# Expert stage of an attention and mixture-of-experts block: the transposes of the next block's rows before the second product instead of inside it

## The reference

```python
gate_probs = jax.nn.softmax(x @ Wg + bg, axis=-1)
_, top_idx = jax.lax.top_k(gate_probs, 2)
...
h = jax.nn.gelu(jnp.einsum('bsf,efh->bseh', x, W1) + b1)
expert_out = jnp.einsum('bseh,ehf->bsef', h, W2) + b2[None, None]
return jnp.einsum('bsef,bse->bsf', expert_out, selected)
```

## Time and profile before

| | |
|---|---|
| median of 3 runs | 966.51 us (966.34 to 971.07) |
| the profiled execution's own time | 965.11 us |
| its span, first to last instruction | 963.4 us |
| mean granted TensorE clock | 0.928 of full |
| PE busy | 825.7 us, 86% of the span |
| DVE busy | 572.3 us, 59% |
| ACT busy | 455.7 us, 47% |
| POOL busy | 276.9 us, 29% |
| chain that ended last, by engine | PE 71%, DVE 12%, POOL 5%, issue 5%, DMA 3% |
| loads of `listed` | 38, of 265.0 KB, 3.0 us to landing (median) |

### The profile page before, as it was taken

How to read it: one execution, slowest core, us unless ns; L and a number is a source line. 1 busy time by engine, 2 the same in 40 slices (tenths; PEclk the granted TensorE clock), 3 DMA queues, 4 the chain that set the end, 5 groups by cost and what they waited for, 6 DMA issues and landing times.

```text
span 963.4 us, 17833 instructions
## 1 busy us (share of the span) xinstructions
PE 825.7 (86%) x5866; PEld 765.9 (80%) x5867; DVE 572.3 (59%) x1365; ACT 455.7 (47%) x876; POOL 276.9 (29%) x206
## 2 busy tenths in 40 slices
PE   5757999999998869864049999999998999999995
PEld 4545888888886757664049999999998999999995
DVE  4768677777777436886016565556656565565553
ACT  4343555665543420111036565747457575665552
POOL 1222223322321012277713222222222222232222
PEclk9979999999998987875569999999999999999998
DMA  8601101101100096643632425152242524322222
GB/s 288 221 0 45 40 5 46 44 1 45 45 1 1 1 348 223 236 153 107 228 108 62 115 40 132 27 132 44 44 131 44 131 44 115 61 45 44 44 45 33
DMA packets 51260, 84.77 MB, mean 88 GB/s; under 512 B 4498, under 2 KB 35668, under 8 KB 51092
## 3 DMA queue, kind: packets, MB, share of 16 engines
q1 hardware_dynamic: 37396, 65.62, 20.1%
q0 software_dynamic: 13824, 18.65, 10.8%
HBM read 50.86 MB, written 33.40 MB: 87 GB/s over the span
## 4 chain that ended last, share of the span: by engine, by line
PE 71%; DVE 12%; POOL 5%; issue 5%; DMA 3%; ACT 1%; SPq 1%; DVEq 0%; ACTq 0%; POOLq 0%
PE ps L1318 20%; PE ps L1306 16%; PE ps L1147 9%; PE ps L1112 8%; PE ps L1166 6%; POOL lists L539 4%; PE ps L1223 3%; PE ps L1156 3%; PE ps L1289 2%; DVE w_lo L1054 2%; DMA listed<-lists 2%; DMA wmod_sb<-in_L_wmod 1%; PE ps L1217 1%; DVE w_lo L1051 1%; DVE ln_s L766 1%
## 5 line engine op out<-in xcount | busy, mean ns | idle before, releaser
L559 POOL DMA_INDIRECT out<-y,y_id x74 | 122.2, 1651 | 349.1 <-DVE y L1043 334.7
L1318 PE MATMUL ps<-w_hi,hid_hi 128*128 128x256 f32 x592 | 171.2, 289 | 12.2 <-DVE hid_lo L1034 12.2
L715 ACT ACTIVATE hid<-ps,b_col 128x256 f32<-128x256 f32 x296 | 122.2, 464 | 113.0 <-PE ps L1306 112.9
L1034 DVE TENSOR_TENSOR hid_lo<-hid,hid_hi 128x512 fp32r<-128x512 f32 x148 | 100.6, 692 | 117.8 <-ACT hid_hi L723 116.4
L1306 PE MATMUL ps<-xT_hi,w_hi 128*128 128x256 f32 x592 | 167.5, 283 | 2.3 <-DVE xT_lo L1015 2.3
L1306 PE MATMUL ps<-xT_lo,w_hi 128*128 128x256 f32 x592 | 167.3, 283 | 0.0
L1306 PE MATMUL ps<-xT_hi,w_lo 128*128 128x256 f32 x592 | 167.2, 282 | 0.0
L1318 PE MATMUL ps<-w_hi,hid_lo 128*128 128x256 f32 x592 | 166.1, 281 | 0.0
L1318 PE MATMUL ps<-w_lo,hid_hi 128*128 128x256 f32 x592 | 166.1, 281 | 0.0
L1318 PEld LDWEIGHTS ps<-w_hi,hid_hi 128*128 128x128 f32 x592 | 112.1, 189 | 15.6 <-DVE hid_lo L1034 14.7
L514 POOL TENSOR_TENSOR q_n<-q_exp,q_rec 128x1024 f32<-128x1024 f32 x32 | 61.0, 1906 | 218.3 <-DVE q_rec L790 218.3
(11 more groups left out here) (190 smaller groups left out, 1491.4 us busy)
## 6 DMA issues: line engine op xcount, KB each, us to landing
w_raw<-in_L_ffn_W SPq DMA_DIRECT2D x16, 1024.0 KB, 8.8
listed<-lists SPq DMA_DIRECT2D x38, 265.0 KB, 3.0
h_store<-h_q SPq DMA_DIRECT2D x8, 1024.0 KB, 4.0
h_b<-h_store SPq DMA_DIRECT2D x16, 512.0 KB, 6.2
x_all<-in_L_attn_x SPq DMA_DIRECT2D x8, 512.0 KB, 11.0
x_b<-in_L_attn_x SPq DMA_DIRECT2D x4, 1024.0 KB, 10.4
out<-x SPq DMA_DIRECT2D x8, 512.0 KB, 3.2
lists<-pad SPq DMA_DIRECT2D x8, 265.0 KB, 2.4
```

The costliest lines, as they stand in the source:

```text
L559: pool.indirect_dma_start(out[:, :], bass.IndirectOffsetOnAxis(ap=y_id[:, i:i + 1], axis=0), y[:, i, :], None, compute_op=ALU.add).then_in ...
L715: ins = act.activation(hid[:, m, :], ps[:, k, (m % 2) * BT:(m % 2 + 1) * BT], ACT.Gelu_apprx_tanh, bias=b1_col[:, bass.ds(e, 1), m])
L1034: dve.tensor_tensor(hid_lo[:, m, :], hid[:, m, :], hid_hi[:, m, :].bitcast(F32), ALU.subtract).then_inc(s_hid, 1)
L1318: last = pe.matmul(ps[:, Y0 + i, 0:D], a, w, start=m == 0 and st, stop=m == M - 1 and sp_)
```

## The change

On PE alone, `block_T(gv + 1)` moves up by one call: it stands between the first and the second product, where it stood behind the first 18 matmuls of the second product.

```diff
@@ -1320,8 +1320,8 @@
                             last.then_inc(s_f2, 1)
 
 
+                    block_T(gv + 1)
                     second(0, range(0, M - 2))
-                    block_T(gv + 1)
                     second(1, range(0, M - 2))
                     second(0, range(M - 2, M))
                     second(1, range(M - 2, M))
```

## The result

The changed kernel takes 994.15 us (median of 4 runs, 992.17 to 998.0) against 966.42 us for the kernel before (4 runs). The ratio is 1.028, with a 95% interval of 1.024 to 1.033: slower by 27.7 us. The forecast was 995.0 us.

The account below looks back on a forecast made before the run. PE was taken to bound the expert stage (443.8 of 456.9 us busy). The sum was 965.1 + 14.9 - 1.3 + 1.7 + 13.2 = 993.6 us, with 1.4 us to the median 995.0 us, range 981 to 1003 us.

Parts of the forecast that it names:

- What can be lost: Expert stage: all that moving PE's instructions can win or lose is in the 13 us in which PE stands still.
- Ordinary blocks, taken as 0: 22 ordinary blocks: the rows land 0.6 us before the transposes are due, so nothing waits: 0, upper bound 2 us.
- Held matmuls, +14.9 us: Seven second blocks: 18 matmuls wait behind the transposes for the rows' landing, 2.12 us each, +14.9 us.
- First blocks, -1.3 and +1.7 us: Eight first blocks: transposes fill gaps in three, 0.44 us each (-1.3 us); rows land late in five others (+1.7 us).
- The clock, +13.2 us: Seven second blocks: the longer gap drops the clock to 1.2 GHz for 4.2 us, 1.9 us each, +13.2 us.
- the 45% of the prediction: At the low clock matmuls come at 0.214 us against 0.118, so 45% of each low stretch is lost.
- The rival in which the clock holds: Second blocks' gaps leave the clock up, so its +13.2 us falls away: 981.8 us; chance 0.17.
- The rival on the other side: Second blocks' rows land before `hid_lo`, so transposes fill gaps in ten blocks: 4.4 us less, 962.1 us; chance 0.03.
- the ten blocks: Seven second blocks and three first blocks with gaps, where the transposes would save 0.44 us each.

Follow-up runs that it names:

- the control: PE's code for each expert's first two blocks written out ahead of the loop, transposes in the old place, against the kernel before: 967.32 us, ratio 1.0015.

## Why the prediction was right

**What can be lost.** The first paragraph says that all that can be won or lost is in the 13 us in which PE stands still. That bounds the gain only; the sum itself goes past it, and the stage lost 31 us.

**Ordinary blocks, taken as 0.** Right in size: 0.6 us in 22 blocks, and the kernel with the new place everywhere but in second blocks is level with the kernel before. The reason was not complete. The margin of 0.6 us was worked out for a load that goes out as early as in the earlier trace rows, and only a slow load was thought to use it up; in two blocks the load goes out over 1 us later, behind a late add of `y`, and PE waits.

**Held matmuls, +14.9 us.** Right. With the clock held up by extra matmuls, the stage is 15.0 us longer than before, and the seven second blocks 2.1 us each, where 2.12 was forecast. The landing did set the start of the transposes, at the distance from `listed_id` that the earlier trace rows showed. In the profiled execution of the changed kernel the idle time grew by 18.6 us, 3.3 us more than the 14.9 - 1.3 + 1.7 = 15.3 of the sum. Most of this is known: 0.7 us are the waits of the two ordinary blocks, about 1 us is the one load that took 4.08 us (the other six took 2.60 to 3.17 us, as before), and about 1 us moved from busy to idle by counting alone. The seven gaps are 3.5 to 5.0 us, a little wider than the 3.7 to 4.2 named, and PE's wait for these landings is 28.6 us, where about 27 was named.

**First blocks, -1.3 and +1.7 us.** The net of 0.4 was forecast, 0.9 us was found: -1.3 as forecast in the three blocks with gaps, and +2.2 in the five others. Six of the eight wait for the rows, 0.15 to 0.54 us, so the worst cost less than the 0.9 worked out and the others more than 0.2 on average. The transposes fill the gaps as described.

**The clock, +13.2 us.** Right in kind and size: all seven gaps brought it down, PE's busy time grew by 12.5 us (about 1 us more without the shift in counting named above), and the comparison with and without extra matmuls gives 13.4 us of time and 14.1 us of stage. The term was read from gaps in other stages of the trace, where the work is of another kind; it held here. The forecast of 4.2 us for each low stretch stands against 2.8 to 5.9 us seen, with a mean of 4.5; at the 45% of the prediction the 31.3 us in all make 14.1. That the middle of four values from 3.4 to 6.7 us came so near is in part luck. The rival in which the clock holds would have given 981.8 us; the kernel in which it was made to hold is 13.4 us below the same kernel without the extra matmuls, where forecast and rival stand 13.2 us apart.

The sum was 995.0 us for the median; 994.15 us was measured. To come within 0.9 us is luck as well: the four runs spread from 992.17 to 998.0 us, and in the traces the stage grew by 31.2 us in the changed kernel but by 26.0 us in the kernel with the new place in second blocks alone, since low stretches and landings differ from one execution to the next.

**The rival on the other side** named its point rightly: with SP's issue ahead of `w_lo` the new place is the faster one. Its price of 4.4 us is what the ten blocks gained; the other 1.6 of the 6.0 us of stage are mostly one fall of the clock that only the kernel with the old place had.

## What to carry to other kernels

- Before moving work on an in-order engine to where it would fill a gap, look up when its input lands in each kind of loop iteration. Here 30 of 37 blocks cared little, and the seven that did were those in which another engine's extra work delayed the request for the input.
- A wait is cheapest where the least work stands behind it. If it makes TensorE idle for some microseconds, count the clock as well: here it was as dear as the wait.
- The fix was not in the place of the transposes, but on DVE: acknowledge a buffer before long work, and cut that work up. Then the place mattered by some 2 us only, which is no more than the measurement can tell.

## What the runs showed of the hardware that was not expected

Short gaps do not act alike, and much shorter ones than the prediction had in mind can be followed by the low clock. With gaps between 2.0 and 3.1 us in the kernel with 12 extra matmuls, three of seven were, the shortest of them a gap of 2.11 us and not the one of 2.86 us. In the control, whose matmuls and waits are those of the kernel before, one second block waits 1.76 us for `hid_lo`; 1.4 us after PE resumed the clock fell, between matmuls that stood close on both sides of the gap (columns as in the earlier trace rows):

```profile
742.40:745.80 3.40, 3.40 (x19) 3.40 (x18) 0.41 (x2) 0.68 (x2) 0.00 (x0) 0.50 0.10 39
```

The same followed a gap of 1.76 us in the kernel with the new place everywhere but in second blocks, and the one of 1.90 us above; gaps of 1.67, 1.70, 1.77 and 1.87 us in these kernels were not followed by it. At 3.4 to 5.0 us all 28 were, in the four traces that have the new place in second blocks and no extra matmuls. Such a fall, with 3.4 us at the low clock, costs 1.5 us, so it is also part of what makes two executions of one kernel differ.

Chips differ more than the change is worth. Of the four that ran the experiments, three run the kernel before in 996 to 998 us and one in 967. The traces put the difference ahead of the expert stage: its first matmul starts at 524 to 526 us on the slower ones and at 494 to 497 us on the other, while the stage itself is about as long (for the changed kernel 485.0 us on a slower chip, 487.8 us on a faster one). The clock's last fall ahead of the stage comes at 416 to 419 us on the slower ones and at 421 to 422 us on the other, so the 30 us arise between there and the stage. Part of the way is seen: the last of POOL's 64 writes of rows into the lists (L539) starts at 498 to 500 us in three traces of slower chips and at 483 to 484 us on the other, and the first load of `listed` goes out at 515 to 516 us against 489 to 490. Why the chips differ there stays open.
